# A decoder layer on one core: every call of four engines written in a new order in head, round and tail

## The chip, the cores and the metric

The kernel runs on one core of a Trainium2 chip. The metric is the device time of one execution in microseconds, the median of several. A core has five engines that run their own instruction streams in parallel: TensorE (PE), VectorE (DVE), ScalarE (ACT), GpSimd (POOL) and SyncE (SP), which here only issues transfers. They meet at semaphores: an instruction raises one when it is done, another engine waits until it has a value.

## The reference, cut to what matters

x is (4, 1024, 256), the context (4, 77, 256), all float32, and all matrices 256 x 256.

```python
# 1 self attention, sigmoid instead of softmax, q and k normalised
q, k, v = x @ Wq.T + bq, x @ Wk.T + bk, x @ Wv.T + bv
a = sigmoid(ln(q) @ ln(k).T / sqrt(256) - log(1024))
x = ln(x + ((a @ v) @ Wo.T + bo) * layerscale)
# 2 cross attention, 16 heads of 16, over 77 rows of context
p = softmax(heads(x @ wq + b) @ heads(ctx @ wk + b).T / 4)
x = ln(x + (p @ heads(ctx @ wv + b)) @ dense + b)
# 3 mix with the row before, receptance, squared keys
xp = x shifted by one row
r = sigmoid((mu_r * x + (1 - mu_r) * xp) @ W_r.T)
kk = square(relu((mu_k * x + (1 - mu_k) * xp) @ W_k.T))
out = ln(x + r * (kk @ W_v.T))
```

## The kernel before, in words

**Work and tiles.** The 4096 rows are 16 pairs of tiles (`NJ` = 16 pairs of 256 rows, `NT` = 32 tiles of 128). Self attention runs in 64 blocks of scores (`NS`), 16 for each batch. Most products are split: each operand is a high and a low half in fp32r, and `split_product` (L291) makes three matmuls of each, so that one such call on TensorE is twelve matmuls of 128x256 or six of 128x512. PSUM banks are few, and each call waits until those who read its bank before are done.

**Calls.** Each engine has one small function for each step, with its waits inside. The calls that the change and the text below speak of are:

- TensorE: `warm_up` (L1886) on zeros; `on_all_rows` (L1890), which spreads a row of biases over 128 partitions; `first_qk` (L1897), `qk` (L1929), `wvo` (L1918), the products q and k, and Wv times Wo; `tqk` (L1957), four transposes of normalised q and k; `scores` (L1971) and `attend` (L1985), twelve matmuls each; `v`, `values` (L2010); `x1` (L2022), `query` (L2030), `cross_scores` (L2039), `weights_t` (L2063, ten transposes of a tile's weights in three parts 0 to 2), `mixed` (L2076) and `dense` (L2095) of cross attention; `x2` (L2106), `receptance` (L2120), `mix_keys` (L2135) and `mix_values` of part 3.
- ScalarE: `qk_biases` (L498) and `fold_biases` (L502), which copy what `on_all_rows` made; `first_x_hi` (L484), `sigmoid` (L543), `sigmoid_hi` (L552), `exponentials` (L583, four heads a call), `mixed_hi` (L601), `query` (L575), `norm2` (L608), `v_hi` (L528). Between sigmoids and exponentials a table is loaded.
- VectorE: `first_x_lo` (L1305), `wqk_lo` (L1301), `qk_bias` (L1324), `qk_norm` (L1341, its last addition is L1347), `attended` (L1367), `stats1` (L1372), `values_bias` (L1391), `mixed_lo` (L1435), `mixes`, `mix_lo` (L1484), `gated`, `stats3` (L1508). Every low half is made at L1294.
- GpSimd: `qk_deviation` (L968), `deviation1`, `normalise` (L1045, of a tile's weights), `fold_weights`, and the like.

A chain of cross attention for one pair is: `cross_scores`, maxima (VectorE), `exponentials` (ScalarE), sums (GpSimd and VectorE), `normalise` (GpSimd), `weights_t`, copies, `mixed`, `mixed_hi` and `mixed_lo`, `dense`, then a residual and a norm.

**Order.** No scheduler is at work: each engine runs its calls in the order in which they are written. There is a head of single calls, then `for r in range(NJ): round_(r)`, in which each line is guarded by `at` (L370), so that its index must lie between two bounds, then a tail of single calls with a short loop `mix_round`. A round is one pair at every stage at once: the scores of pair r beside cross attention of pair r - 7 and q and k of tiles 2r and 2r + 1. The two lines of `at` are

```python
def at(call, i, count=NJ, first=0, *more):
    if first <= i < count:
        call(i, *more)
```

## Time and profile before

| | |
|---|---|
| three runs | 533.92, 534.5, 535.41 us; median 534.5 |
| profiled execution | 533.92 us, span of the trace 532.1 us |
| mean granted TensorE clock | 0.997 of full |
| instructions in the trace | 12650 |

The profile is of one of the runs, the fastest. Its span runs from the first to the last instruction on the core, and 1.8 us of the execution lie around it. A page gives the share of each engine; the trace behind it has every instruction with start, duration and, in brackets, the idle time of its engine just before it and the instruction that ended it. A matmul's bracket is small also where it started late, since its neighbours overlap.

### The profile page before, as it was taken

The numbers are of one execution on the slowest core, as the hardware profiler recorded it, in microseconds if no ns is written. First come the engines' busy times: TensorE is split into PE (matmuls) and PEld (weight loads), VectorE is DVE, ScalarE is ACT, GpSimd is POOL, SyncE is SP. The second block draws the span as 40 slices with busy tenths as digits, with TensorE's granted clock in tenths as the row PEclk, the third lists the DMA queues.
The fourth block names the chain that finished last, engine by engine and source line by source line (L and its number), as shares of the span: only waits on it lengthen the run. The fifth ranks groups of instructions, "written<-read, shape, count | busy, mean of one in ns | idle before, by whom it ended". The sixth has DMA issues, their size and how long they took to land.

```text
span 532.1 us, 12650 instructions
## 1 busy us (share of the span) xinstructions
PE 514.3 (97%) x4530; PEld 468.4 (88%) x4530; DVE 443.4 (83%) x995; ACT 442.7 (83%) x1070; POOL 381.6 (72%) x554
## 2 busy tenths in 40 slices
PE   9999899999999999999999999999999898999994
PEld 6799899898989898989898989999898787899994
DVE  4788868878888879797979797778878888999996
ACT  3665479897989898989898979888998799898965
POOL 1784748666857575767667675767778889897996
PEclk9999999999999999999999999999999999999998
DMA  6410010110011010101010100020601000011122
GB/s 193 127 54 30 26 60 6 41 40 2 19 44 31 30 41 22 43 19 53 10 39 2 40 2 21 21 78 24 196 5 41 2 1 1 22 41 42 41 80 100
DMA packets 23267, 22.49 MB, mean 42 GB/s; under 512 B 1723, under 2 KB 23203, under 8 KB 23204
## 3 DMA queue, kind: packets, MB, share of 16 engines
q1 hardware_dynamic: 22770, 21.35, 12.6%
q8 instruction: 36, 0.59, 0.5%
q10 hardware_dynamic: 434, 0.34, 0.2%
q14 instruction: 27, 0.22, 0.2%
HBM read 14.55 MB, written 6.82 MB: 40 GB/s over the span
## 4 chain that ended last, share of the span: by engine, by line
PE 74%; DVE 10%; ACT 8%; issue 4%; POOL 3%; POOLq 0%; DVEq 0%; ACTq 0%
PE st L296 17%; PE acc L296 15%; PE xb L296 10%; PE proj L296 9%; PE xb L2072 6%; PE xb L2091 5%; PE xb L2059 4%; DVE xm L1480 3%; ACT p_sb L590 3%; PE proj L1968 2%; PE xb L1880 1%; POOL rs L1105 1%; DVE xmT_lo L1294 1%; PE st L1888 1%; DVE kkT_lo L1294 1%
## 5 line engine op out<-in xcount | busy, mean ns | idle before, releaser
L590 ACT ACTIVATE p_sb<-xb,neg_mx 128x77 f32<-128x77 f32 x512 | 120.0, 366 | 7.7 <-DVE neg_mx L1407 7.1
L1042 POOL TENSOR_TENSOR fold<-p_sb 128x640 f32<-128x640 f32 x32 | 50.9, 1592 | 75.6 <-ACT p_sb L590 75.5
L1047 POOL TENSOR_TENSOR p_sb<-p_sb,rc 128x1280 f32<-128x1280 f32 x32 | 75.2, 2351 | 24.5 <-DVE rc L1420 24.3
L541 ACT ACT_TABLE_LOAD x58 | 74.4, 1283 | 3.2 <-issue 2.2
L296 PE MATMUL acc<-vv_hi,aT_hi 128*128 128x256 f32 x256 | 76.6, 299 | 0.0
L296 PE MATMUL st<-qkT_hi 128*128 128x256 f32 x256 | 74.8, 292 | 0.0
L296 PE MATMUL st<-qkT_lo,qkT_hi 128*128 128x256 f32 x256 | 72.4, 283 | 0.0
L296 PE MATMUL st<-qkT_hi,qkT_lo 128*128 128x256 f32 x256 | 72.4, 283 | 0.0
L296 PE MATMUL acc<-vv_lo,aT_hi 128*128 128x256 f32 x256 | 72.2, 282 | 0.0
L296 PE MATMUL acc<-vv_hi,aT_lo 128*128 128x256 f32 x256 | 72.2, 282 | 0.0
L1407 DVE TENSOR_REDUCE neg_mx<-xb 128x4 f32<-128x308 f32 x128 | 53.7, 468 | 18.0 <-PE xb L2059 17.6
L549 ACT ACTIVATE a_sb<-st,nlogs 128x512 f32<-128x512 f32 x64 | 43.7, 687 | 16.8 <-PE st L296 16.2
L296 PEld LDWEIGHTS st<-qkT_hi 128*128 128x128 f32 x256 | 48.9, 191 | 4.8 <-issue 4.2
L1427 DVE COPY pT<-xb 128x512 f32<-128x512 f32 x64 | 43.1, 676 | 11.0 <-PE xb L2072 10.9
L296 PEld LDWEIGHTS acc<-vv_hi,aT_hi 128*128 128x128 f32 x256 | 48.6, 190 | 3.4 <-issue 3.3
L2072 PE MATMUL xb<-columns,p_sb 128*128 128x128 f32 x320 | 48.4, 274 | 2.0 <-DVE pT L1427 0.6
L1294 DVE TENSOR_TENSOR aT_lo<-a_sb,aT_hi 128x512 fp32r<-128x512 f32 x64 | 47.7, 746 | 2.6 <-ACT aT_hi L475 2.2
L296 PEld LDWEIGHTS st<-qkT_lo,qkT_hi 128*128 128x128 f32 x256 | 48.9, 191 | 0.2
L296 PEld LDWEIGHTS st<-qkT_hi,qkT_lo 128*128 128x128 f32 x256 | 48.9, 191 | 0.0
L296 PEld LDWEIGHTS acc<-vv_lo,aT_hi 128*128 128x128 f32 x256 | 48.8, 191 | 0.1
L296 PEld LDWEIGHTS acc<-vv_hi,aT_lo 128*128 128x128 f32 x256 | 48.7, 190 | 0.0
L475 ACT ACTIVATE aT_hi<-a_sb 128x512 fp32r<-128x512 f32 x64 | 43.2, 678 | 2.6 <-PE acc L296 2.4
(259 smaller groups left out, 1693.1 us busy)
## 6 DMA issues: line engine op xcount, KB each, us to landing
xs<-in_x SPq DMA_DIRECT2D x16, 256.0 KB, 3.2
xraw<-in_xT SPq DMA_DIRECT2D x15, 256.0 KB, 2.9
out_y<-y SPq DMA_DIRECT2D x15, 256.0 KB, 2.1
x_kept<-xs SPq DMA_DIRECT2D x10, 256.0 KB, 2.1
x2s_a<-x_kept SPq DMA_DIRECT2D x2, 512.0 KB, 5.4
x2s_b<-x_kept SPq DMA_DIRECT2D x2, 512.0 KB, 7.2
x2s_c<-x_kept SPq DMA_DIRECT2D x1, 512.0 KB, 3.7
cT<-in_cT SPq DMA_DIRECT2D x1, 308.0 KB, 3.3
```

Source lines behind the costliest of these rows:

```text
L296: mm = pe.matmul(out, s_, m_, start=first and k == 0 and q == 0, stop=last and k == n - 1 and q == 2, skip_group_check=not check)
L475: return act.activation(out, in_, ACT.Identity, **kw)
L541: act.preload_act_table(func)
L549: act.activation(a_sb[:, i % NAR], st_bank[i % 2], ACT.Sigmoid, bias=nlogs[:, 0:1], scale=1.0 / 16).then_inc(sg_act.sem, 1)
L590: ex = act.activation(weights(t)[:, h // KH * (H // 2) + KH * n + h % KH, 0:SC], logits[n][:, h * SC:(h + 1) * SC], ACT.Exp, bias=neg_mx[: ...
L1042: pool.tensor_tensor(fold[:].rearrange("p (h k) -> p h k", k=FO), p[:, :, 0:FO], p[:, :, FO:2 * FO], ALU.add).then_inc(fo_pool.sem, 1)
L1047: pool.tensor_tensor(weights(t), weights(t), rc[:, t % 2].rearrange("p (h o) -> p h o", o=1) .to_broadcast([P, H, SP]), ALU.mult).then_inc ...
L1294: return dve.tensor_tensor(lo, whole, f(hi), ALU.subtract)
L1407: dve.tensor_reduce(neg_mx[:, t % 2, HG * n:HG * (n + 1)], logits[n][:, 0:HG * SC].rearrange("p (h k) -> p h k", k=SC), AX, ALU.min)\
L1427: dve.tensor_copy(pT[:, 4 * c:4 * c + 4, (t % 2) * P:(t % 2 + 1) * P], tiles(tp_bank(c), 4))\
L2072: mm = pe.transpose(tp_bank(c)[:, (n - 4 * c) * P:(n - 4 * c + 1) * P], p_sb[:, t % NP, n * P:(n + 1) * P], ident)
L2091: mm = pe.matmul(mixed_bank(i)[32 * n:32 * (n + 1), k * D:(k + 1) * D], vb[:, n, half, :, :, KC * b + k].rearrange("p a d -> p (a d)"), pT ...
```

## The change

No call is added, removed or altered on any engine; the functions are the same text, and SyncE's block is untouched. The order of the calls is new, in all three stretches. The head and the tail are rewritten on four engines. `at` is no longer used: `round_` has plain calls and is run for fewer rounds (TensorE 7 to 13, ScalarE 6 to 11, GpSimd 6 to 12, VectorE 5 to 10), and what lay in the rounds before and after, and in `mix_round`, is written out call by call. The cut of a round against the other engines and the order in it are new as well.

On TensorE the head begins as follows (`st`, `xb` are PSUM tiles, `brow` the row of biases, `a_sb` holds zeros in the warm-up). Before:

```order
L1888 MATMUL st<-a_sb 128x256 x4
L1888 MATMUL st<-a_sb 128x128
L1901 MATMUL xb<-wqk_hi,xT_hi 128x512 x2
L1901 MATMUL xb<-wqk_hi,xT_lo 128x512 x2
L1901 MATMUL xb<-wqk_lo,xT_hi 128x512 x2
```

The change (the same function is 285 lines further down in its file):

```order
L2173 MATMUL st<-a_sb 128x256 x4
L2173 MATMUL st<-a_sb 128x128
L2179 MATMUL st<-brow,ones 128x512 x2
L2186 MATMUL xb<-wqk_hi,xT_hi 128x512 x2
L2186 MATMUL xb<-wqk_hi,xT_lo 128x512 x2
L2186 MATMUL xb<-wqk_lo,xT_hi 128x512 x2
```

Both `on_all_rows` now stand ahead of `first_qk`; before, one came behind it and the other after `qk(3)`.

On ScalarE, in the same place (`bqk` is written by `qk_biases`, `ls` and `bo` by `fold_biases`, `xT_hi` and `wqk_hi` are high halves). Before:

```order
L541 ACT_TABLE_LOAD
L703 DMA columns<-in_columns 128x136
L475 ACTIVATE xT_hi<-xraw 128x256 x2
L475 ACTIVATE wqk_hi<-wraw 128x512
L475 ACTIVATE xT_hi<-xraw 128x512
L475 ACTIVATE bqk<-st 128x512
```

The change:

```order
L541 ACT_TABLE_LOAD
L695 DMA columns<-in_columns 128x136
L475 ACTIVATE bqk<-st 128x512
L475 ACTIVATE xT_hi<-xraw 128x256
L475 ACTIVATE ls<-st 128x256
L475 ACTIVATE bo<-st 128x256
L475 ACTIVATE xT_hi<-xraw 128x256
L475 ACTIVATE wqk_hi<-wraw 128x512
L475 ACTIVATE xT_hi<-xraw 128x512
```

The copies of biases have moved ahead of the halves of x and of the weights.

On TensorE around `mixed(13)`, at 420 us of the trace of before (`pT` are transposed weights, L2091 is `mixed`, L2059 `cross_scores`, the rows with `xmT` and `wf` are the first three of `mix_keys(0)`). Before:

```order
L2091 MATMUL xb<-pT,vb 32x256 x16
L2059 MATMUL xb<-kb,xq 128x154 x8
L296 MATMUL st<-xmT_hi,wf_hi 128x256
L296 MATMUL st<-xmT_lo,wf_hi 128x256
L296 MATMUL st<-xmT_hi,wf_lo 128x256
```

The change (L2357 is `weights_t`, L2165 the transposes of `x2(1)`, L2376 `mixed`):

```order
L2357 MATMUL xb<-columns,p_sb 128x128 x10
L2165 MATMUL proj<-columns,x2s_a 128x128 x4
L2376 MATMUL xb<-pT,vb 32x256 x16
L296 MATMUL st<-xmT_hi,wf_hi 128x256
L296 MATMUL st<-xmT_lo,wf_hi 128x256
L296 MATMUL st<-xmT_hi,wf_lo 128x256
```

`cross_scores(29)` now follows behind all twelve matmuls of `mix_keys(0)`.

The diff, cut to the places above and those that the prediction speaks of: the head and the round of ScalarE, the end of VectorE's tail, and of TensorE the round, the head, the stretches around `tqk(9)`, `weights_t(0, .)` and `mixed(13)`.

```diff
                 def round_(r):
-                    at(xt_hi, r + 3, NJ, 9)
-                    at(weights_tail, 2 * r - 9, NTA, 3)
-                    at(sigmoid, 4 * r - 7, NS, 16)
-                    at(mixed_hi, r - 5, NJ, 1)
-                    at(sigmoid, 4 * r - 6, NS, 16)
-                    at(exponentials, 2 * r - 7, NT, 4, 0)
-                    at(exponentials, 2 * r - 7, NT, 4, 1)
-                    at(exponentials, 2 * r - 7, NT, 4, 2)
-                    at(sigmoid_hi, 4 * r - 7, NS, 16)
-                    at(exponentials, 2 * r - 7, NT, 4, 3)
-                    at(norm1, r - 3, N1, 3)
-                    at(sigmoid_hi, 4 * r - 6, NS, 16)
-                    at(tqk_hi, 2 * r + 4, NT, 15)
-                    at(x1_hi, r - 3, NJ, 3)
-                    at(sigmoid, 4 * r - 5, NS, 16)
-                    at(v_hi, r + 2, NJ, 7)
-                    at(norm2, r - 6, N2)
-                    at(weights_tail, 2 * r - 8, NTA, 3)
-                    at(sigmoid, 4 * r - 4, NS, 16)
-                    at(query, r - 3, NJ, 2)
-                    at(sigmoid_hi, 4 * r - 5, NS, 16)
-                    at(exponentials, 2 * r - 6, NT, 4, 0)
-                    at(exponentials, 2 * r - 6, NT, 4, 1)
-                    at(sigmoid_hi, 4 * r - 4, NS, 16)
-                    at(exponentials, 2 * r - 6, NT, 4, 2)
-                    at(tqk_hi, 2 * r + 5, NT, 15)
-                    at(exponentials, 2 * r - 6, NT, 4, 3)
-
-                def mix_round(i):
-                    at(key_squares, i - 1, NJ, 22)
-                    at(mix_hi, i + 1, NJ, 24)
-                    at(key_relu, i, NJ, 22)
-                    at(gate_sigmoid, i - 1, NJ, 19)
-                    at(carried, i + 7, NJ, 17)
-
+                    exponentials(2 * r - 7, 1)
+                    exponentials(2 * r - 7, 2)
+                    norm1(r - 3)
+                    exponentials(2 * r - 7, 3)
+                    tqk_hi(2 * r + 4)
+                    sigmoid_hi(4 * r - 6)
+                    x1_hi(r - 3)
+                    sigmoid(4 * r - 5)
+                    norm2(r - 6)
+                    weights_tail(2 * r - 8)
+                    sigmoid_hi(4 * r - 5)
+                    v_hi(r + 2)
+                    query(r - 3)
+                    sigmoid(4 * r - 4)
+                    exponentials(2 * r - 6, 0)
+                    exponentials(2 * r - 6, 1)
+                    sigmoid_hi(4 * r - 4)
+                    exponentials(2 * r - 6, 2)
+                    tqk_hi(2 * r + 5)
+                    xt_hi(r + 4)
+                    exponentials(2 * r - 6, 3)
+                    weights_tail(2 * r - 7)
+                    sigmoid(4 * r - 3)
+                    sigmoid_hi(4 * r - 3)
+                    mixed_hi(r - 4)
+                    sigmoid(4 * r - 2)
+                    exponentials(2 * r - 5, 0)
...
                 table_for(ACT.Sigmoid)
                 act.dma_start(columns[:], io["columns"]).then_inc(load_id.sem, 16)
+                qk_biases()
                 first_x_hi(0)
+                fold_biases()
                 first_x_hi(1)
                 wqk_hi(1)
                 xt_hi(1)
-                qk_biases()
                 xt_hi(2)
-                fold_biases()
                 qk_norm(0)
+                wvo_hi()
                 tqk_hi(0)
+                xt_hi(3)
                 qk_norm(1)
-                wvo_hi()
-                xt_hi(3)
...
-                for r in range(NJ):
...
+                for r in range(6, 12):
                     round_(r)
...
                 mixes(14)
-                key_squares_lo(11)
-                stats3(9)
+                key_squares_lo(12)
                 mix_lo(14)
-                gated(10)
+                stats3(10)
                 gated(11)
-                stats3(10)
-                key_squares_lo(12)
+                key_squares_lo(13)
+                gated(12)
+                mixes(15)
+                mix_lo(15)
                 stats3(11)
-                mixes(15)
-                gated(12)
-                key_squares_lo(13)
-                mix_lo(15)
                 key_squares_lo(14)
                 gated(13)
                 stats3(12)
                 gated(14)
+                stats3(13)
                 key_squares_lo(15)
-                stats3(13)
@@ -2164,281 +2449,327 @@
                     mm.then_inc(fv_pe.sem, 1)
 
                 def round_(r):
-                    at(attend, 4 * r - 18, NS, 9)
-                    at(scores, 4 * r - 15, NS, 13)
-                    at(weights_t, 2 * r - 13, NT, 1, 0)
-                    at(tqk, 2 * r - 1, NT, 13)
-                    at(weights_t, 2 * r - 13, NT, 1, 1)
-                    at(attend, 4 * r - 17, NS, 9)
-                    at(weights_t, 2 * r - 13, NT, 0, 2)
-                    at(qk, 2 * r, NT, 14)
-                    at(mixed, r - 7)
-                    at(scores, 4 * r - 14, NS, 13)
-                    at(cross_scores, 2 * r - 11, NT, 2)
-                    at(v, r, NJ, 7)
-                    at(scores, 4 * r - 13, NS, 13)
-                    at(scores, 4 * r - 12, NS, 13)
-                    at(dense, r - 7)
-                    at(weights_t, 2 * r - 12, NT, 1, 0)
-                    at(tqk, 2 * r, NT, 13)
-                    at(x1, r - 5, NJ, 2)
-                    at(attend, 4 * r - 16, NS, 9)
-                    at(qk, 2 * r + 1, NT, 14)
-                    at(weights_t, 2 * r - 12, NT, 1, 1)
-                    at(weights_t, 2 * r - 12, NT, 0, 2)
-                    at(query, r - 5, NJ, 1)
-                    at(attend, 4 * r - 15, NS, 9)
-                    at(cross_scores, 2 * r - 10, NT, 2)
-
-                def mix_round(i):
-                    at(mix_keys, i - 3, NJ, 12)
-                    at(mix_values, i - 5, NJ, 14)
-                    at(receptance, i - 3, NJ, 14)
-                    at(x2, i, NJ, 18)
...
-
+                    weights_t(2 * r - 13, 0)
+                    tqk(2 * r - 1)
+                    weights_t(2 * r - 13, 1)
+                    attend(4 * r - 17)
+                    weights_t(2 * r - 13, 2)
+                    qk(2 * r)
+                    mixed(r - 7)
+                    scores(4 * r - 14)
+                    cross_scores(2 * r - 11)
+                    v(r)
+                    scores(4 * r - 13)
+                    scores(4 * r - 12)
+                    dense(r - 7)
+                    tqk(2 * r)
+                    weights_t(2 * r - 12, 0)
+                    x1(r - 5)
+                    weights_t(2 * r - 12, 1)
+                    attend(4 * r - 16)
+                    qk(2 * r + 1)
+                    weights_t(2 * r - 12, 2)
+                    query(r - 5)
+                    attend(4 * r - 15)
+                    cross_scores(2 * r - 10)
+                    attend(4 * r - 14)
+                    scores(4 * r - 11)
 
                 warm_up()
+                on_all_rows(0)
+                on_all_rows(1)
                 first_qk()
-                on_all_rows(0)
                 qk(2)
                 qk(3)
-                on_all_rows(1)
+                wvo()
+                tqk(0)
                 qk(4)
-                tqk(0)
...
+                attend(3)
+                scores(5)
                 values(1)
-                tqk(8)
-                keys(1)
-                scores(4)
-                qk(9)
-                attend(1)
-                attend(2)
-                attend(3)
+                scores(6)
                 tqk(9)
-                scores(5)
+                scores(7)
                 qk(10)
-                scores(6)
+                x1(0)
                 v(5)
-                scores(7)
-                x1(0)
...
+                cross_scores(1)
                 scores(10)
                 qk(12)
-                cross_scores(1)
-                attend(7)
                 scores(11)
                 v(6)
+                weights_t(0, 0)
+                attend(8)
+                weights_t(0, 1)
+                x1(1)
+                tqk(12)
+                attend(9)
+                query(1)
+                weights_t(0, 2)
+                qk(13)
                 scores(12)
-                attend(8)
-                tqk(12)
-                weights_t(0, 0)
-                x1(1)
-                weights_t(0, 1)
-                qk(13)
-                for r in range(NJ):
+                cross_scores(2)
+                scores(13)
+                attend(10)
+                for r in range(7, 14):
                     round_(r)
+                weights_t(15, 0)
...
                 cross_scores(28)
-                x2(1)
-                attend(62)
+                attend(63)
                 weights_t(27, 0)
                 weights_t(27, 1)
                 weights_t(27, 2)
-                attend(63)
+                x2(1)
                 mixed(13)
+                mix_keys(0)
                 cross_scores(29)
-                mix_keys(0)
                 receptance(0)
-                dense(13)
-                x1(15)
                 weights_t(28, 0)
                 weights_t(28, 1)
-                x2(2)
+                x1(15)
+                dense(13)
                 query(15)
                 weights_t(28, 2)
+                x2(2)
...
```

## Rows read from the trace of the kernel before

**Rows 1.** The page, part 1: busy time, share of the span, instructions of each engine.

```profile
PE 514.3 (97%) x4530; PEld 468.4 (88%) x4530; DVE 443.4 (83%) x995; ACT 442.7 (83%) x1070; POOL 381.6 (72%) x554
```

**Rows 2.** 20 us windows: us; busy (x instructions) PE, PEld, DVE, ACT, POOL; PEclk, DMA, GB/s.

```profile
40.00:60.00 20.00, 18.57 (x131) 16.80 (x130) 16.43 (x31) 8.39 (x15) 10.54 (x18) 1.00 0.11 35
...
420.00:440.00 20.00, 16.64 (x167) 14.26 (x166) 16.64 (x40) 16.05 (x53) 17.77 (x23) 1.00 0.01 2
...
500.00:520.00 20.00, 18.90 (x152) 18.12 (x151) 18.79 (x44) 15.37 (x31) 18.97 (x33) 1.00 0.20 67
520.00:532.00 12.00, 5.08 (x41) 4.73 (x39) 7.16 (x23) 6.49 (x12) 7.64 (x17) 0.87 0.32 110
```

**Rows 3.** Chain of waits: start us, us, what; `mixed` in it.

```profile
103.15 1.90 PE xb L2091 x32
...
129.05 1.90 PE xb L2091 x32
...
336.41 1.90 PE xb L2091 x32
...
420.35 1.94 PE xb L2091 x32
```

**Rows 4.** Timeline around `tqk(9)`, TensorE, then VectorE: start us, us, operation, [idle before <-releaser].

```profile
55.06 0.28 PE L296 MATMUL acc<-vv_lo,aT_hi 128*128 128x256 f32 x1
55.18 0.28 PE L296 MATMUL acc<-vv_hi,aT_lo 128*128 128x256 f32 x1
56.80 0.44 PE L1968 MATMUL proj<-columns,qk_sb 128*128 128x128 f32 x2 [1.35 <-DVE qk_sb L1347]
...
51.19 0.69 DVE L1329 TENSOR_TENSOR qk_sb<-proj,bqk 128x512 f32<-128x512 f32 x1 [1.43 <-PE proj L296]
...
52.80 1.11 DVE L1395 TENSOR_TENSOR v<-xb,bxv 77x256 f32<-77x256 f32 x2
```

**Rows 5.** Timeline of TensorE from `mixed(13)` on.

```profile
423.78 0.81 PE L2059 MATMUL xb<-kb,xq 32*128 32x154 f32 x16 [1.53 <-DVE oT_lo L1294]
424.52 0.39 PE L296 MATMUL st<-xmT_hi,wf_hi 128*128 128x256 f32 x1
...
429.49 0.60 PE L1880 MATMUL xb<-columns,xs 128*128 128x128 f32 x4
...
434.13 0.81 PE L2059 MATMUL xb<-kb,xq 32*128 32x154 f32 x16 [0.72 <-ACT xq L475]
```

**Rows 6.** Head: timeline of TensorE, then the tiles `brow` and `wraw`.

```profile
5.18 1.19 PE L1901 MATMUL xb<-wqk_hi,xT_hi 128*128 128x512 f32 x2
...
8.74 1.12 PE L1894 MATMUL st<-brow,ones 1*128 1x512 f32 x2
...
18.60 0.58 PE L296 MATMUL xb<-wqk_hi,xT_first_hi 128*128 128x512 f32 x1
...
L701 ACTq DMA_DIRECT2D brow<-in_brow x1: 537/537/537, 1.6 to 1.6; - x1
...
DMA to landing us min/median/max: 3.0/3.5/4.3
```

**Rows 7.** Line L1347, the last addition of `qk_norm`: ns min/median/max.

```profile
L1347 DVE TENSOR_TENSOR qk_sb<-qk_sb,nb x26: 691/693/1762, 32.6 to 331.3; 128x512 f32<-128x512 f32 x26
```

**Rows 8.** Timeline of ScalarE and TensorE before `cross_scores` in a repeated round.

```profile
275.00 0.84 ACT L475 ACTIVATE xq<-xb,columns 128x256 f32<-128x256 f32 x2
...
276.31 0.81 PE L2059 MATMUL xb<-kb,xq 32*128 32x154 f32 x16
```

**Rows 9.** Timeline of TensorE, `weights_t` behind a `cross_scores` that starts at 350.96.

```profile
353.80 0.41 PE L2072 MATMUL xb<-columns,p_sb 128*128 128x128 f32 x2 [0.41 <-ACT p_sb L590]
```

**Rows 10.** Timeline of VectorE in the tail.

```profile
513.61 0.74 DVE L1515 BATCH_NORM_STATS2 st<-y 128x6 f32<-128x256 f32 x2
514.27 0.30 DVE L1520 BATCH_NORM_AGGREGATE mv<-st 128x2 f32<-128x6 f32 x2
...
517.28 1.28 DVE L1294 TENSOR_TENSOR xmT_lo<-xm,xmT_hi 128x512 fp32r<-128x512 f32 x2
```

More of the change, by code:

```diff
@@ new lines, in _ @@
+                tqk_hi(29)
+                sigmoid(45)
+                weights_tail(17)
+                v_hi(14)
+                norm2(6)
+                sigmoid(46)
+                sigmoid_hi(45)
+                mixed_hi(8)
+                norm1(10)
+                sigmoid_hi(46)
+                exponentials(19, 0)
+                exponentials(19, 1)
+                exponentials(19, 2)
+                exponentials(19, 3)
+                x1_hi(10)
+                tqk_hi(30)
+                sigmoid(47)
@@ L810, in _ @@
+                exponentials(24, 1)
+                exponentials(24, 2)
+                exponentials(24, 3)
                 sigmoid(57)
@@ L812, in _ @@
                 sigmoid_hi(57)
+                sigmoid(58)
+                sigmoid_hi(58)
                 exponentials(25, 0)
@@ new lines, in _ @@
+                tqk(28)
+                weights_t(16, 1)
+                dense(7)
+                weights_t(16, 2)
+                x1(9)
+                scores(44)
+                attend(41)
+                query(9)
+                qk(29)
+                cross_scores(18)
+                scores(45)
+                attend(42)
+                weights_t(17, 0)
+                attend(43)
+                tqk(29)
+                weights_t(17, 1)
+                weights_t(17, 2)
+                scores(46)
@@ L2272, in _ @@
+                qk(30)
+                mixed(8)
+                v(15)
+                attend(44)
+                cross_scores(19)
+                scores(47)
+                scores(48)
+                weights_t(18, 0)
+                attend(45)
+                x1(10)
+                weights_t(18, 1)
+                tqk(30)
+                weights_t(18, 2)
+                dense(8)
+                query(10)
+                qk(31)
+                cross_scores(20)
                 attend(46)
+                weights_t(19, 0)
@@ L2300, in _ @@
                 mixed(10)
-                attend(52)
+                scores(54)
                 cross_scores(23)
```

1141 lines of the change are left out of this document (718 added, 423 removed).

## Prediction

> **What bounds the kernel now.** I read the page's engine shares first: TensorE is busy 97% of the span, no other engine over 83% [rows 1]. A new order removes no work, so it can only remove time in which TensorE stands still. The 20 us windows say where: 1.43 us at 40 to 60, 3.36 at 420 to 440, 1.10 at 500 to 520, and 6.92 in the last 12 us, where TensorE's work thins out [rows 2]. In the chain of waits the same call, `mixed`, comes back after 25.9 us (103.15 to 129.05): that is the repeated round [rows 3].
>
> The windows understate the standstill. A matmul of 0.28 us is followed by the next after 0.12, so twelve take 1.44, and each late start hides 0.16 us under the matmul before: `tqk(9)` starts 1.62 us after the last matmul of `attend(3)`, and shows 1.35 idle [rows 4]. Between `mixed(9)` (336.41) and `mixed(13)` (420.35) lie 83.9 us [rows 3]. Their calls at full pace: 37 of twelve matmuls, 53.3; 4 `mixed`, 7.6; 8 `cross_scores` at 0.74 (423.78 to 424.52), 5.9; 22 sets of four transposes at 0.44 (0.60 busy less the 0.16 under the next) and 8 pairs at half of it, 11.4 [rows 5]; some 0.18 for each of 12 changes to and from mixed or cross_scores, 2.1; less 0.4, since dense and query are a little shorter. That is 79.9, so 4 us are waiting though the windows show far less. Summed in this way over the program, waiting comes to some 19 us beside the start and the last 7 us.
>
> The Trainium skill (Perfetto Trace Analysis, Identifying the Most-Contended Engine) calls matmul busy time a poor measure of headroom and asks for the weight-load share instead. Here that share is 88%, which would leave 12% or 64 us; the pace of 0.12 us per matmul leaves a third of that, and I go by the pace.
>
> **The change, part by part.** The same calls stand on every engine, with 58 table loads as before, so added work costs nothing. The sum is made against the profiled execution, 533.9 us (span 532.1), which is 0.6 below the median of 534.5.
>
> *Head, to 20 us.* Both `on_all_rows` (1.05 us each; the first is 8.74 to 9.79) move ahead of `first_qk` on TensorE, and on ScalarE the two bias copies go ahead of the halves of x. The row they need (`brow`) is issued at 1.6; the weights on the same queue took 3.0 to 4.3 us to land, so it is there by 5.9 at worst, against 5.18, the end of the warm-up [rows 6]. TensorE then starts `first_qk` at about 7.3, not 5.18. VectorE now makes both low halves of x before the low part of the first weights, and has the second weights' low part at about 10.1, so `first_qk` ends at about 10.7 instead of 8.74. The 2.1 us of `on_all_rows` are by then done, as is the wait for the first biases. Adding `qk(2)`, `qk(3)`, `wvo`, `tqk(0)` and `qk(4)` at full pace (1.4, 1.4, 2.5, 0.45, 1.5) gives 18.0; before, that set ended at 18.60 [rows 6]. Gain 0.5 (bounds -0.7, if the row lands at its worst, and 1.2). Between 20 and 50 us half of some 0.7 of small waits may go: 0.3.
>
> *tqk(9).* It waited for `qk_norm(9)`: VectorE takes the result of `qk(9)` at 51.19, 0.2 us after TensorE ends it, and `tqk(9)` starts at 56.80, so 5.8 us after `qk(9)` [rows 4]. Before, 4.3 us of attend covered this; now `attend(3)`, `scores(5)`, `values(1)` and `scores(6)` do, 4 x 1.44 and the changes between them, 6.2 us. On VectorE `attended(0)` and `stats1(0)` come into the chain (some 1.6 us, one addition and the statistics at the paces of this stretch) and `values_bias(0)` (1.1) leaves it. One of the 26 last additions of `qk_norm` took 1.76 where 0.69 is usual, and it is the one that TensorE waited for [rows 7]. So the chain is 6.3 us with the slow addition, 5.2 with a usual one. So 0 to 0.1 is left. Gain 1.6 (0.5 to 2). Later `weights_t(0,0)` and `(0,1)` no longer stand so close: a wait of 0.3 goes, an estimate from the sum of standstill at 80 to 100 us.
>
> *Repeated round.* Three rows change places on TensorE (`tqk` before `weights_t(.,0)`, and `weights_t(.,1)` two calls earlier). Nothing waited there, so no gain, and I find nothing new that is late: 0. The least cover is ScalarE's `query` copies, done at 275.84 for `cross_scores` at 276.31, 0.47 us [rows 8].
>
> *336 to 420 us.* Each `cross_scores` is followed by 2.3 us of TensorE work before a `weights_t` that wants its exponentials 2.8 us after its start; at 353.80 this shows as 0.41 idle, so 0.57 late [rows 9]. The new order puts two calls instead of one behind `cross_scores(24)`, `(25)` and `(27)`, and leaves one behind `(22)`, `(26)` and `(28)`. I count 0.6 each as left on those three plus 0.8 of small ones, 2.6 of 4.2: gain 1.6 (0 to 3).
>
> *mixed(13).* `cross_scores(29)` waited 1.53 for the chain mixed, `mixed_hi`, `mixed_lo` [rows 5]. `mix_keys(0)` (1.5) now stands between. But next are `weights_t(28,.)`, moved ahead of `dense(13)`, which want `normalise(28)` and `exponentials(29,1)`. With the normalise two small groups earlier on GpSimd these come some 5.3 and 4.8 us after mixed's end, TensorE is there after 3.9: 1.4 comes back. `dense(13)` then covers the halves of x1. I reach `cross_scores(30)` 10.9 us after mixed's end instead of 11.95 (422.18 to 434.13): gain 1.1 (0 to 3).
>
> *Tail.* VectorE is busy 18.79 of 20 us at 500 to 520, TensorE 18.90 [rows 2]: the two set the pace together, and VectorE's work is unchanged. What can go is order: `stats3(11)` (0.74 and 0.30, at 513.61) moves behind `mix_lo(15)` (517.28), which `mix_keys(15)` waits for [rows 10], 1.0 us sooner. With the last 7 us as before: gain 1.2 (0 to 3.5).
>
> Sum: 0.5 + 0.3 + 1.6 + 0.3 + 1.6 + 1.1 + 1.2 = 6.6. 533.9 - 6.6 is 527.3; the runs' median is 0.6 above the profiled run, so half a microsecond more: **527.8 us**.
>
> **Rivals.**
> - *Waits come back later.* ScalarE and VectorE set the pace from 340 us on, so TensorE, sooner at one call, waits at the next. For: VectorE's 18.79 us from 500. Against: ScalarE idles 4.0 us and VectorE 3.4 at 420 to 440 [rows 2]. Only the first 100 us gain: 2.7, so 531.7.
> - *Nearly all waits go.* The upper ends of the bounds: 1.2 + 0.7 + 2 + 0.3 + 3 + 3 + 3.5 = 13.7, so 520.7.
> - *No change.* The order does little: counts per round are equal, and head and tail give back what tqk(9) gains. 533 to 535.
> - *Slower: the round's cover fails.* ScalarE's order around `v_hi`, `norm2` and `query` is new. If the query copies end over 0.47 us later, each of ten rounds stands still. If they end 1.3 us later, 0.85 a round is lost and ten rounds cost 8.5: 6.6 is eaten up and 1.9 added, 536.3. It decides from 0.8 of standstill a round, where the sum passes the 533.9 of before by over 1.6. For: the small cover. Against: the copies swapped (`sigmoid_hi` for `sigmoid`) last the same.
> - *Slower: VectorE beside GpSimd.* One addition in 26 took 1.07 us more than the median of 0.69 [rows 7]. If the new order lays eight more such subtractions and additions beside GpSimd's work, where TensorE waits for them, 8 x 1.07 = 8.6 cancels the gain: 536.4. For: nothing in the order says which way the pairs fall. Against: the one that TensorE waited for goes or stays alone, and elsewhere the cover is over 1 us. The Trainium skill (SBUF — State Buffer, Who interferes with whom) has the second port as an exclusive lock for VectorE instructions with two SBUF inputs against GpSimd's reads. By that rule this time is one instruction waiting for the other; the slow one agrees with it.
>
> **How the numbers follow.** About 0.3%, 1.6 us, is what a measurement of this kernel can tell from no change, so faster is below 532.9. Forecast 0.53, waits come back 0.20, nearly all go 0.05 (all faster, 0.78); no change 0.13; the query copies 0.05, VectorE beside GpSimd 0.04 (slower, 0.09). Eight in ten: from 522.8 (between forecast and the low rival) to 533.0 (past the first rival).
>
> **What would show it.** Right: TensorE's idle at 40 to 60 us near 0.2; the round still 25.9 us; `cross_scores(29)` without wait but `weights_t(28,0)` with one of about a microsecond; `mixed(13)` 3.5 to 5 us earlier than 420.3; 7 us still behind the last matmul. Wrong: a round of 26.2 or more, a `first_qk` ending after 11.5, or VectorE with more busy time than 443 us. The forecast falls if the sum of waiting from 420 on is unchanged.

## The result and the profile after

| | before | the change |
|---|---|---|
| median of 4 runs each | 534.21 us (533.58 to 535.41) | **542.05 us** (540.68 to 542.84) |
| ratio | | 1.0141, 95% interval 1.0110 to 1.0173 |
| profiled execution, span | 533.92, 532.1 | 542.83, 541.0 |

The change is 1.4% slower. I had forecast 527.8 us, 1.2% faster, with a chance of 0.09 for slower: direction and range were both wrong.

Part 1 of the page of the changed kernel, in answer to [rows 1]:

```profile
PE 517.9 (96%) x4530; PEld 470.4 (87%) x4530; DVE 455.8 (84%) x995; ACT 442.8 (82%) x1070; POOL 383.9 (71%) x554
```

The number of instructions on each engine is the same, and VectorE is busy 12.4 us longer with them. The prediction named more than 443 us on VectorE as a sign against it.

Windows of the changed kernel (columns as in [rows 2]):

```profile
0.00:20.00 20.00, 17.25 (x42) 11.47 (x43) 9.02 (x21) 5.67 (x11) 4.60 (x15) 1.00 0.42 128
...
40.00:60.00 20.00, 20.00 (x152) 18.97 (x151) 15.47 (x29) 9.11 (x16) 16.13 (x17) 1.00 0.14 41
420.00:440.00 20.00, 17.83 (x177) 15.64 (x176) 18.45 (x43) 16.86 (x53) 18.42 (x19) 1.00 0.08 27
500.00:520.00 20.00, 20.00 (x168) 19.80 (x168) 19.80 (x50) 18.23 (x39) 19.11 (x36) 1.00 0.15 53
```

Where the change was meant to help, at 40 to 60 and at 500 to 520, TensorE has no idle time left. The loss lies where I had put nothing. The chain of waits, whose pieces of `mixed` answer to [rows 3]:

```profile
106.57 1.90 PE xb L2376 x32
...
132.58 1.90 PE xb L2376 x32
...
158.46 1.89 PE xb L2376 x32
...
185.28 1.90 PE xb L2376 x32
...
212.11 1.89 PE xb L2376 x29
...
238.94 1.90 PE xb L2376 x32
...
265.78 1.90 PE xb L2376 x32
...
292.64 1.90 PE xb L2376 x32
```

The round lasts 26.0 and 25.9 us at first, then 26.8: some 0.9 more in each of five rounds. Standstill summed as in the prediction, by the start of each call less the full pace of its kind, gives the account (us, the change less before):

| stretch | predicted | measured |
|---|---|---|
| head, to the end of `qk(4)` (18.60 before, 23.68 now) | -0.5 | +5.1 |
| from there to 160 | -2.2 | -1.3 |
| 160 to 340, the repeated rounds | 0 | +6.1 (6.2 against 0.1) |
| 340 to 460 | -2.7 | +0.5 (11.7 against 11.2) |
| 460 to the last matmul | -1.2 | -1.0 (3.0 against 4.1) |
| last matmul to the end | 0 | -0.1 |

The rows add up to 9.3, against 8.9 in the spans. Of the 6.1 in the rounds 4.6 are the five rounds of 26.8; the rest lies at 300 to 340. Some 0.7 of it is `tqk(28)`, which waits for the last such addition: from `mixed(7)` to `mixed(8)` the change takes 28.2 us, and 27.5 with that addition short (e1 below). For the other half of the rest no cause is shown.

**A round of the changed kernel.** The timeline of VectorE, GpSimd, ScalarE, and of TensorE without its split matmuls:

```profile
192.24 0.68 DVE L1478 TENSOR_TENSOR qk_sb<-qk_sb,rs 128x512 f32<-128x512 f32 x1
192.96 1.82 DVE L1480 TENSOR_TENSOR qk_sb<-qk_sb,nb 128x512 f32<-128x512 f32 x1
194.70 0.68 DVE L1427 TENSOR_TENSOR aT_lo<-a_sb,aT_hi 128x512 fp32r<-128x512 f32 x1
195.31 0.46 DVE L1540 TENSOR_REDUCE neg_mx<-xb 128x4 f32<-128x308 f32 x1
...
192.40 0.58 POOL L1091 TENSOR_TENSOR nbl<-nbl,rsl 128x2 f32<-128x2 f32 x1
192.93 1.29 POOL L1056 TENSOR_TENSOR xT_lo<-xraw,xT_hi 128x512 fp32r<-128x512 f32 x1
...
195.80 0.97 ACT L590 ACTIVATE p_sb<-xb,neg_mx 128x77 f32<-128x77 f32 x4 [1.29 <-DVE neg_mx L1540]
...
195.70 0.60 PE L2357 MATMUL xb<-columns,p_sb 128*128 128x128 f32 x4
196.92 0.63 PE L2165 MATMUL xb<-columns,xs 128*128 128x128 f32 x4 [0.62 <-ACT p_sb L590]
```

GpSimd's `nbl`, of 128x2, takes 0.58 instead of 0.20: it ends when VectorE's L1478 ends. GpSimd then starts `xt_lo` (L1056) 0.03 us ahead of VectorE's next addition, and that takes 1.82 instead of 0.69: it ends 0.56 after GpSimd's instruction. The two engines hand each other the turn, and they meet like this, 0.02 to 0.03 us apart, in six rounds; in a seventh GpSimd came second. Behind the slow addition now stand a low half of scores and `maxima(., 3)` (L1540); ScalarE waits 1.29 us for it, and `x1` on TensorE starts 0.79 us late. Before, `maxima(., 3)` stood ahead of `qk_norm`, and `xt_lo` behind `residual2`.

Line L1480 in the changed kernel, against [rows 7], says the same of its longest; seven of the 26 took 1.67 to 1.82:

```profile
L1480 DVE TENSOR_TENSOR qk_sb<-qk_sb,nb x26: 691/693/1822, 36.5 to 342.0; 128x512 f32<-128x512 f32 x26
```

**The head.** TensorE, VectorE and GpSimd in the changed kernel, against [rows 6]:

```profile
5.31 3.78 PE L2179 MATMUL st<-brow,ones 1*128 1x512 f32 x4
9.02 1.22 PE L2186 MATMUL xb<-wqk_hi,xT_hi 128*128 128x512 f32 x2
10.04 1.05 PE L2186 MATMUL xb<-wqk_hi,xT_lo 128*128 128x512 f32 x2
12.67 1.22 PE L2186 MATMUL xb<-wqk_lo,xT_hi 128*128 128x512 f32 x2 [1.58 <-DVE wqk_lo L1427]
13.69 1.05 PE L2186 MATMUL xb<-wqk_hi,xT_hi 128*128 128x512 f32 x2
...
10.12 0.83 DVE L1427 TENSOR_TENSOR xT_lo<-xraw,xT_hi 128x256 fp32r<-128x256 f32 x1 [1.34 <-ACT xT_hi L475]
10.87 2.35 DVE L1427 TENSOR_TENSOR wqk_lo<-wraw,wqk_hi 128x512 fp32r<-128x512 f32 x2
...
10.62 1.44 POOL L1048 TENSOR_TENSOR wo_ls<-wo_ls,ls 128x512 f32<-128x512 f32 x1
```

Three things come together: each `on_all_rows` takes 1.85 us and not 1.05; the second half of x waits on ScalarE behind both bias copies; and the low half of the weights, late by that, meets GpSimd's fold of the output weights (L1048): two low halves take 2.35 us, where two of this size elsewhere take 1.3. The matmuls come 0.43 to 0.51 us apart (0.85 to 1.02 for two), up to the start of `qk(2)` at 16.25, where before they came 0.23 apart from 6.8 on. 512 columns in 0.43 us is the level of 1.2 GHz, in 0.23 that of 2.4. In this profile the column of the granted clock shows 1.00 in all of the stretch and does not tell the two apart; in e7, e6 and e2 below it shows 0.50 where the matmuls come 0.43 apart.

### The profile page after: what moved, and what is told of

It is laid out like the page before. It is cut to its first block, busy times and chain, and to the rows that moved or that the text cites. A ratio compares the mean times of both kernels' runs of the same rounds, so it can differ in the third digit from the quotient of the medians.

```text
span 541.0 us, 12658 instructions
## 1 busy us (share of the span) xinstructions
PE 517.9 (96%) x4530; PEld 470.4 (87%) x4530; DVE 455.8 (84%) x995; ACT 442.8 (82%) x1070; POOL 383.9 (71%) x554
## 3 DMA queue, kind: packets, MB, share of 16 engines
q1 hardware_dynamic: 22770, 21.35, 12.5%
## 4 chain that ended last, share of the span: by engine, by line
PE 80%; DVE 10%; issue 4%; ACT 3%; POOL 2%; DMA 1%; POOLq 0%; DVEq 0%; ACTq 0%
PE st L296 19%; PE acc L296 18%; PE xb L296 12%; PE proj L296 8%; PE xb L2357 5%; PE xb L2376 5%; PE xb L2344 4%; DVE neg_mx L1540 2%; PE xb L2165 2%; PE proj L2253 2%; ACT p_sb L590 1%; DVE aT_lo L1427 1%; DVE pT L1560 1%; PE st L2173 1%; DVE v_sb L1493 1%
## 5 line engine op out<-in xcount | busy, mean ns | idle before, releaser
L590 ACT ACTIVATE p_sb<-xb,neg_mx 128x77 f32<-128x77 f32 x512 | 117.4, 361 | 15.3 <-DVE neg_mx L1540 15.0
L1137 POOL TENSOR_TENSOR p_sb<-p_sb,rc 128x1280 f32<-128x1280 f32 x32 | 75.2, 2351 | 27.5 <-DVE rc L1553 27.5
L1540 DVE TENSOR_REDUCE neg_mx<-xb 128x4 f32<-128x308 f32 x128 | 55.4, 467 | 16.3 <-PE xb L2344 15.7
L2357 PE MATMUL xb<-columns,p_sb 128*128 128x128 f32 x320 | 49.4, 274 | 4.7 <-DVE pT L1560 1.9
L1427 DVE TENSOR_TENSOR aT_lo<-a_sb,aT_hi 128x512 fp32r<-128x512 f32 x64 | 53.0, 829 | 0.2 <-ACT aT_hi L475 0.2
L2357 PEld LDWEIGHTS xb<-columns,p_sb 128*128 128x128 f32 x320 | 37.0, 140 | 8.3 <-DVE pT L1560 2.9
```

Of the source, the lines that this page charges most:

```text
L590: ex = act.activation(weights(t)[:, h // KH * (H // 2) + KH * n + h % KH, 0:SC], logits[n][:, h * SC:(h + 1) * SC], ACT.Exp, bias=neg_mx[: ...
L1137: pool.tensor_tensor(weights(t), weights(t), rc[:, t % 2].rearrange("p (h o) -> p h o", o=1) .to_broadcast([P, H, SP]), ALU.mult).then_inc ...
L1427: return dve.tensor_tensor(lo, whole, f(hi), ALU.subtract)
L1540: dve.tensor_reduce(neg_mx[:, t % 2, HG * n:HG * (n + 1)], logits[n][:, 0:HG * SC].rearrange("p (h k) -> p h k", k=SC), AX, ALU.min)\
L2357: mm = pe.transpose(tp_bank(c)[:, (n - 4 * c) * P:(n - 4 * c + 1) * P], p_sb[:, t % NP, n * P:(n + 1) * P], ident)
```

## The experiments

Each is the changed kernel, or the kernel before, with a few calls moved; no call is added, and none computes anything else. The kernel before was run beside them each time: medians 534.2, 534.12 and 533.75 us.

**e1: GpSimd's `xt_lo` back.**

```diff
                     deviation1(r - 3)
-                    xt_lo(r + 3)
                     fold_weights(2 * r - 7)
                     deviation2(r - 6)
                     residual2(r - 4)
+                    xt_lo(r + 3)
```

> The changed kernel, with xt_lo(r + 3) in GpSimd's round moved from behind deviation1 to behind residual2, where it stood before. Theory port: in the changed kernel xt_lo starts 0.02 to 0.03 us ahead of VectorE's last addition of qk_norm, which then takes 1.82 us instead of 0.69; maxima(., 3) stands behind it, then exponentials(., 3), then TensorE's x1, which starts 0.79 us late in six rounds. With xt_lo later the addition takes 0.69 again and the wait before x1 is gone: about 4.6 us less, 542.05 to 537.4; from 160 to 300 us TensorE's standstill falls from 4.7 to under 1 us. Rival order: x1 waits because ScalarE's and VectorE's order in the round put the exponentials late, whatever GpSimd does: no change, 542. Rival later: xt_lo behind residual2 makes q and k late instead: over 542.

Measured 537.24 us, 4.8 less than the change. The longest L1480 is 0.818 us, the round lasts 25.9, and of TensorE's waits at 160 to 330 us (3.1 for the exponentials before `x1`, 0.3 for the addition) none is left. Rows of e1, VectorE:

```profile
191.37 0.68 DVE L1478 TENSOR_TENSOR qk_sb<-qk_sb,rs 128x512 f32<-128x512 f32 x1
192.08 0.69 DVE L1480 TENSOR_TENSOR qk_sb<-qk_sb,nb 128x512 f32<-128x512 f32 x1
```

**e2: VectorE's `maxima(., 3)` back, GpSimd as changed.**

```diff
                     maxima(2 * r - 3, 2)
+                    maxima(2 * r - 3, 3)
                     qk_norm(2 * r + 8)
                     sigmoid_lo(4 * r + 1)
-                    maxima(2 * r - 3, 3)
```

> The changed kernel, with maxima(., 3) in VectorE's round put ahead of qk_norm and of the low half of the scores, where it stood before; GpSimd as in the changed kernel. Theory port with an exposed place: the addition of qk_norm still takes 1.8 us in some six rounds, but nothing that TensorE waits for stands behind it in the next microsecond: x1 on time, 537.4. Theory port alone (every such collision costs its 1.1 us wherever it lies): 542. If the low half of the scores, which now is late, is what attend wants, the wait only changes its place: 540 to 543.

Measured 536.74 us. Six additions are as slow as before the edit, and `x1` no longer waits behind them: the round lasts 25.9 us. Of the waits for an addition only that of `tqk(28)` stays, 0.6. Rows of e2, VectorE, GpSimd and TensorE:

```profile
191.18 1.67 DVE L1480 TENSOR_TENSOR qk_sb<-qk_sb,nb 128x512 f32<-128x512 f32 x1
...
190.51 1.80 POOL L1056 TENSOR_TENSOR xT_lo<-xraw,xT_hi 128x512 fp32r<-128x512 f32 x1
...
193.98 0.60 PE L2165 MATMUL xb<-columns,xs 128*128 128x128 f32 x4
```

Here GpSimd came second to L1478 (190.47) and took 1.80 instead of 1.29, then VectorE came second to it. So in these rounds a collision costs only where something due stands behind it: e1 takes the collision away, e2 its victim, and either is enough.

**e3: the head back.**

```diff
 tensor
-                on_all_rows(0)
-                on_all_rows(1)
                 first_qk()
+                on_all_rows(0)
+                on_all_rows(1)
 scalar
-                qk_biases()
                 first_x_hi(0)
-                fold_biases()
                 first_x_hi(1)
                 wqk_hi(1)
                 xt_hi(1)
+                qk_biases()
+                fold_biases()
 vector
                 first_x_lo(0)
-                first_x_lo(1)
                 wqk_lo(0)
+                first_x_lo(1)
```

> The changed kernel, with the bias copies of ScalarE behind the high halves of x and of the weights, both on_all_rows behind first_qk on TensorE, and VectorE's first low halves in the order of before. All else as changed. Theory head: the order in the first 20 us costs 5.1 us (the set of calls up to qk(4) ends at 23.7 instead of 18.6) and nothing behind takes it back: first_qk starts at 5.2, ends at 8.7, 542.05 becomes 537. Rival slack: what is won in the head is waited for at 30 to 70 us, where q, k and the norms limit: 540 to 542.

Measured 537.69 us, 4.4 less than the change. `qk(2)` starts at 10.55 and not 16.25, `mixed(0)` at 100.99 and not 106.50: the change never made the head's loss good, and what is won back reaches the end: the spans of the two profiled executions differ by 5.8 us. The medians differ by 4.4 only; the last section has a reason why they may fall short, TensorE's pace in the head.

**e7: as e3, but `on_all_rows` stays first on TensorE.** The edit is e3 without its first part, so ScalarE's and VectorE's calls go back together, and what each of them does is not told apart.

> As e3, but both on_all_rows stay ahead of first_qk on TensorE; ScalarE's and VectorE's order in the head as before. Theory ScalarE's queue: what cost the head was that the halves of x waited behind the bias copies; with those behind, only the matmuls of on_all_rows themselves stand in front: first_qk starts at 7.5 to 9.0, runs without a gap, qk(2) starts at 11 to 12.5, and the time is 538 to 539. Theory TensorE's pace: matmuls stay at the slow pace until late, as in the changed kernel (qk(2) at 16.25), because of what TensorE did first: first_qk from 9.0 at 0.5 us a matmul, ends at 14.2, time 541.

Measured 538.73 us, 1.0 more than e3, 3.3 less than the change; `qk(2)` starts at 11.23. So the larger part of the head's loss is the order on ScalarE and VectorE with what follows from it, and by the medians 1 us is TensorE's. Its four runs lie apart, though (537.66, 537.88, 539.59, 540.40), and the profile is of that of 537.88. TensorE in e7, then the window from 8 to 11 us:

```profile
4.88 1.98 PE L2179 MATMUL st<-brow,ones 1*128 1x512 f32 x4
6.79 0.73 PE L2186 MATMUL xb<-wqk_hi,xT_hi 128*128 128x512 f32 x2
7.36 0.68 PE L2186 MATMUL xb<-wqk_hi,xT_lo 128*128 128x512 f32 x2
7.84 1.06 PE L2186 MATMUL xb<-wqk_lo,xT_hi 128*128 128x512 f32 x2
...
8.00:11.00 3.00, 3.00 (x9) 2.35 (x8) 0.90 (x2) 1.73 (x5) 1.75 (x2) 0.50 0.56 173
```

Its matmuls were 0.24 us apart by 7.4, and from 7.84 to 11.2 again 0.43, without any gap, at a granted clock of 0.50. What stood between the warm-up and the fall were the one-row matmuls of `on_all_rows` and four others. It is not shown that their new place is the cause. In e3, with `first_qk` ahead of them, the pace did not fall; in e6 (below), whose head is that of e3, it fell from 12.23 to 15.2 us, 1.3 us behind the same one-row matmuls. TensorE in e6, then the window from 12.5 to 15 us:

```profile
12.23 0.63 PE L296 MATMUL xb<-wqk_hi,xT_lo 128*128 128x512 f32 x1
12.65 0.63 PE L296 MATMUL xb<-wqk_hi,xT_hi 128*128 128x512 f32 x1
...
12.50:15.00 2.50, 2.50 (x7) 1.91 (x7) 2.21 (x7) 0.00 (x0) 2.42 (x6) 0.50 0.01 4
```

**e4, e12, e11: the two edits of the round in the kernel before,** one by one and together. A 2 by 2 test in a program that has none of the rest of the change.

```diff
 gpsimd (e4, e11)
                     at(deviation1, r - 3, NJ, 1)
+                    at(xt_lo, r + 3, NJ, 7)
...
                     at(residual2, r - 4)
-                    at(xt_lo, r + 3, NJ, 7)
 vector (e12, e11)
                     at(sigmoid_lo, 4 * r - 3, NS, 17)
+                    at(maxima, 2 * r - 5, NT, 4, 3)
...
                     at(stats2, r - 4)
-                    at(maxima, 2 * r - 3, NT, 4, 3)
```

(After the last round `maxima(27, 3)` is called once more by itself.)

> The kernel before, with xt_lo(r + 3) in GpSimd's round put directly behind deviation1, as the change has it; VectorE as before, so with maxima(., 3) ahead of qk_norm. Theory port with an exposed place: one of qk_norm's two operations takes 1.8 us instead of 0.69 in each of some eight rounds, but no wait of TensorE comes of it: 534 to 535. Theory port alone: eight rounds by 0.8 to 1.1, 541 to 543. Rival: GpSimd's order decides nothing, no slow additions, 534.

> The control for e11: the kernel before with VectorE's edit alone. Without the collision maxima(., 3) ends at about 268.5 and the exponentials at 269.6, beside x1 at 269.5: 0 to 0.3 us a round, 534 to 537. Together with e4 (GpSimd's edit alone, 535.98) and e11 this shows whether the two edits cost more together than apart.

> The kernel before with both edits of the round: GpSimd's xt_lo directly behind deviation1, and VectorE's maxima(., 3) behind qk_norm and the low half of the scores that follow it. Theory port with an exposed place: exponentials(., 3), then x1, come later by the whole of it. From the trace of before, maxima(., 3) would end at about 268.5 and not 265.4 without the collision and at 269.6 with it, exponentials 1.1 us after that at 270.7, and x1 is due at 269.5: 1.2 us a round, for the six or seven rounds in which both are there 7 to 8 us: 541 to 543. Rival: the collision does not matter, only VectorE's order: same as e12.

| | GpSimd as before | `xt_lo` early |
|---|---|---|
| VectorE as before | 534.2; round 25.9 | e4: 535.98; round 25.9 |
| `maxima(., 3)` late | e12: 546.55; round 27.1 | e11: 553.07; round 27.6 |

(The round is from `mixed(4)` to `mixed(5)`.) In e4 a collision in every round (the first step of `qk_norm` takes 1.65 instead of 0.70) costs nothing there, as expected; the 1.8 us came at 80 to 140 us, from single waits. Together the edits cost 19.3 us, 4.7 more than apart (1.8 and 12.8). That is the interaction I claim for the change. But the size of e12 was a miss: I had looked for 0 to 0.3 us a round, and it was 1.15; e11, for which I had named 541 to 543, came out 10 us above that for the same reason. I had reckoned with the exponentials alone and left out what stands behind them on ScalarE. In the kernel before that is `norm1`, and `x1` waits for it. TensorE in e12, then in e11, one round each:

```profile
194.63 0.66 PE L1882 MATMUL xb<-columns,xs 128*128 128x128 f32 x4 [0.92 <-ACT xs L475]
```

```profile
199.02 0.66 PE L1882 MATMUL xb<-columns,xs 128*128 128x128 f32 x4 [1.50 <-ACT xs L475]
```

The changed kernel has `norm1` ahead of `exponentials(., 3)`, and the late `maxima` alone (e1) cost it nothing. That the place of `norm1` is why is a reading of the two orders; no run moved it alone.

**e5: e2 and e3 together.**

> The changed kernel with the edits of e2 and e3 together: biases behind the halves of x in the head, maxima(., 3) ahead of qk_norm in the round. If the two causes are independent, their gains add (5.3 and 4.4 us): 532.3, which is under the kernel before. If both gains are one slack in different places (the rounds catch up what the head lost), 536 to 537.

Measured 533.03 us, ratio to before 0.9985 (0.9975 to 0.9995). The two causes are 9.0 us together, 9.7 by their sum: nearly independent (the edit of e2 is worth 5.3 by itself and 4.7 on top of e3). With both undone the rest of the change is worth 1.1 us against the kernel before.

**e6: three swaps on VectorE in the middle.**

```diff
-                rest_of_mu()
                 weights_tail(23)
+                rest_of_mu()
...
+                x1_lo(13)
                 sigmoid_lo(58)
                 crossed(11)
                 weights_tail(24)
-                x1_lo(13)
...
-                wf_split(0)
                 weights_body(25, 0)
                 maxima(26, 3)
                 weights_tail(25)
                 weights_body(25, 1)
+                wf_split(0)
```

> As e5, with three swaps on VectorE at 380 to 410 us: rest_of_mu (1.42 us) behind weights_tail(23) and not ahead of it, x1_lo(13) ahead of the low half of scores 58 and crossed(11), wf_split(0) behind the copies of weights 25. Theory place: TensorE's waits before mixed(11) (0.95), query(13) (1.08) and weights_t(25, 2) (1.0) in e3 are each made by one VectorE operation that nobody needs yet and that stands ahead of one that TensorE waits for: these go, some is waited for later, 2 us less than e5: 530.3. Rival chain: the middle is bound by the chain of cross attention over three engines, and the waits move to the next call: same as e5 within 0.5.

Measured 534.94 us, 1.9 worse than e5. The three waits shrank or went, and TensorE then waited for `xq` (0.8) and 2.1 for one low half, both before a `cross_scores`. In the waits of e6 at 380 to 420 us:

```profile
PE xb L2344 <- DVE oT_lo L1427: 2.1, 1, 2.1
PE xb L2344 <- ACT xq L475: 0.8, 1, 0.8
```

`wf_lo`, moved by the third swap, had met GpSimd's `fold_weights` and taken 1.94 us, and a low half of scores behind it had met `residual2` and taken 1.66. Much of the 1.9 us is not of the middle. In the profiled executions e6 is 2.6 us longer than e5, and 1.4 of that is there at the end of `qk(4)`, in a head of the same code, where the granted clock fell to 0.50. All twelve runs of e6 have a mean granted clock of 0.990 to 0.994; the three runs of e5 that reach only 0.992 to 0.995 took 534.08 to 534.40, against 534.94. So the swaps themselves cost some 0.5 to 1.2 us, and gained nothing: the reading that the waits move is the nearer one. Which of the three swaps did what was not tried.

**e8: the swap around `mixed(13)`, alone, in the kernel before.**

```diff
                 mixed(13)
-                cross_scores(29)
                 mix_keys(0)
+                cross_scores(29)
                 receptance(0)
```

> The kernel before with one swap on TensorE: mix_keys(0) between mixed(13) and cross_scores(29). By my prediction's reading of the change 1.53 us of standstill before cross_scores(29) go and part of it comes back. Theory gain: 1 us less, 533.2. Theory moved: cross_scores(29) starts at 423.7 as before, 1.44 us of work less stands between it and dense(13), which wants its exponentials, and dense(13) waits 1.5 us longer: 534.2, no change, the whole wait moved.

Measured 534.82 us, ratio 1.0017 (1.0007 to 1.0027). TensorE in e8:

```profile
424.13 0.81 PE L2059 MATMUL xb<-kb,xq 32*128 32x154 f32 x16
...
428.33 0.39 PE L296 MATMUL xb<-wx_hi,oT_hi 128*128 128x256 f32 x1 [1.77 <-ACT p_sb L590]
...
434.50 0.81 PE L2059 MATMUL xb<-kb,xq 32*128 32x154 f32 x16 [0.72 <-ACT xq L475]
```

The 1.53 us before `cross_scores(29)` of [rows 5] are gone, and `dense(13)` waits 1.77 instead of 0.31. `cross_scores(30)` starts 12.0 us after the end of `mixed(13)`, as it did before. All of the wait moved.

**e9: e5 with the tail mended.** In the changed kernel the last call of TensorE waits; TensorE and VectorE:

```profile
532.39 0.38 PE L296 MATMUL xb<-wf_hi,kkT_hi 128*128 128x256 f32 x1 [1.87 <-DVE kkT_lo L1427]
...
530.20 0.69 DVE L1637 SCALAR_TENSOR_TENSOR y<-gate,acc 128x512 f32<-128x512 f32 x1 [1.48 <-DMA out_y<-y]
...
531.68 0.66 DVE L1427 TENSOR_TENSOR kkT_lo<-xb,kkT_hi 128x512 fp32r<-128x512 f32 x1
```

```diff
+                key_squares_lo(15)
                 gated(14)
                 stats3(13)
-                key_squares_lo(15)
```

> As e5, with key_squares_lo(15) ahead of gated(14) and stats3(13) at the end of VectorE's tail. In e5 the last call of TensorE, mix_values(15), waits some 1.9 us for that low half, which stands behind gated(14), held by a transfer of y that isn't out. Theory place: mix_values(15) starts at once, and the end is 1.5 to 2 us earlier: 531.3. Rival end: the last rows wait for the norms of rows 12 to 14 on GpSimd and ScalarE or for their transfers, and the end moves under 0.5: 532.7.

Measured 532.43 us, 0.9973 of before (0.9962 to 0.9984), so 0.6 less than e5 by the ratios. `mix_values(15)` starts 2.3 us earlier (520.24), but then the statistics of row pair 14 wait 1.18 us for GpSimd's `y`, and the last norm is only 1 us earlier. Between the two theories, nearer to the second.

**e10: e9 and e1's edit.**

> As e9, with GpSimd's xt_lo(r + 3) behind residual2 as in e1. Slow additions in the rounds fall from 7 to 2, but since maxima(., 3) is out of their way nothing waited for them: theory port with an exposed place says the same time as e9 within 0.5 us, 531.3. Theory port alone says 4 to 6 us less. If a low half of scores was late behind the slow addition at 280 to 300 us (0.87 standstill in e5), 0.9 less: 530.4.

Measured **531.37 us**, 0.9950 of before (0.9937 to 0.9962), 1.1 less than e9: the last reading held as a difference to e9, which itself had come out above its forecast. From `mixed(7)` to `mixed(8)` e9 takes 28.2 us and e10 27.4. It is the fastest kernel of the study, 0.5% under the kernel before and some 10 us under the change, and differs from the change by five moved calls in the head, two in the round and one in the tail.

## Why the prediction was wrong

- **Where TensorE stands still:** right. The account by full pace, made again on the changed kernel, found all of the loss (9.3 us against 8.9 in the spans), also where the windows showed little.
- **Head, predicted -0.5, measured +5.1.** Two steps failed. One is "has the second weights' low part at about 10.1": it was there at 13.2. The second half of x waited on ScalarE behind both bias copies, and then VectorE's low halves met GpSimd's fold, which those copies had started. By e7 this order is the larger part, 3.3 of 4.4 us. The other is the price of both `on_all_rows` and of what follows them. I took 1.05 us from the row at 8.74 [rows 6], which stands at 2.4 GHz; the place they moved to can be at 1.2, as `first_qk` at 5.18 in the same rows shows (1.19 us for two matmuls, against 0.62 later). In the profile of the change each took 1.85, and `first_qk` kept that pace to its end at 16.25, against the 10.7 of the prediction; in those of e2 and e7 they took 1.1 and 0.95. My bound of -0.7 was far too near. e3 undoes the loss: 4.4 us.
- **`tqk(9)`, predicted -1.6 with a range from 0.5 to 2:** right in mechanism. TensorE's idle time at 40 to 60 us is 0.00, where I had named 0.2 as the sign.
- **Repeated round, predicted 0, measured +6.1.** The step: "I find nothing new that is late: 0". I read TensorE's and ScalarE's order there, where the least cover was 0.47 us, and not what VectorE and GpSimd do side by side. The rival "VectorE beside GpSimd" had the mechanism, its price (1.07 us each; here 1.0 to 1.13) and nearly the count (eight; here seven additions of `qk_norm`, and six low halves of scores beside `residual2`), at a chance of 0.04. What I held against it, that elsewhere the cover is over 1 us, was said of the order of before. The new order had taken that cover away by putting `maxima(., 3)` behind. It could have been read from the two orders: two moves on two engines, each of which the changed kernel bears by itself (e1, e2).
- **336 to 420 us and `mixed(13)`, predicted -2.7, measured +0.5.** `cross_scores(29)` does start without wait, and `weights_t(28, 0)` waits 1.62 us, as foretold. The step that failed is "gain 1.1" beside it: e8, the same swap in the kernel before, shows that all of the wait moves. In the stretch ahead of it I counted only calls of TensorE; VectorE's `rest_of_mu` (1.42 us), `wf_split(0)` and a low half of 2.03 us beside GpSimd now stood ahead of what TensorE wanted. That these three are the cause is read from the rows; when e6 moved them, the waits went to other calls and no time was won.
- **Tail, predicted -1.2, measured -1.0:** right in size. Of the standstill at 500 to 520 nothing shows in the window now (idle 1.10 before), and a new wait of 1.87 before `mix_values(15)` takes part of that back.

The signs that I had named against the forecast (a round of 26.2 or more, `first_qk` ending after 11.5, VectorE over 443 us) all came: 26.8, 16.25 and 455.8. `mixed(13)`, foretold 3.5 to 5 us earlier than 420.3, came at 431.75.

## What to carry to other kernels

When an order of several engines is rewritten, check for each engine what now stands directly behind an instruction that can be stretched, and whether someone is due on it: a collision that was harmless under the old order can be exposed by a move on another engine. Take the price of a moved instruction from rows at the place that it moves to, clock included. Count a removed wait as a gain only when the next two calls have been given their due times as well; e8 and e6 show waits of 1 to 2 us that only went to the next call.

## What the runs showed of the hardware

**VectorE and GpSimd take turns.** With additions, subtractions or products of two SBUF tensors on VectorE (`aT_lo`, `xmT_lo`, both steps of `qk_norm`) beside GpSimd's tensor-tensor instructions, the one that starts first keeps its own time, and the other ends some 0.5 us after it. VectorE second: started 0.03, 0.46 and 1.0 us after a GpSimd instruction of 1.29 it took 1.82, 1.38 and 0.84. GpSimd second: the same instruction took 1.74 to 1.80. GpSimd's scalings of one tensor (L1097, L1156 in the change) stretched no such subtraction by more than 0.25. A cast is not safe either: `wf_hi`, with one input in SBUF, took 1.49 us beside `xs<-xs,bo` at 407.1 in the changed kernel, and 0.41 at 428.7. The Trainium skill (SBUF — State Buffer, Who interferes with whom) says that the order of issue decides which engine blocks; every pair looked at here agrees. Then there is the hand-over: a 128x2 instruction of GpSimd that had been held up (0.58 instead of 0.20) set the next one free at the very moment of VectorE's next, round after round.

**TensorE's pace in the head varies between executions with the same head.** In the profiled execution of e2, with the changed head, both `on_all_rows` took 2.2 us together (5.31 to 7.51) and not 3.7, the first matmuls of `first_qk` ran at 2.4 GHz, and after 2.25 us of waiting the next ones, from 10.96 to 15.4, at 1.2 again, with a granted clock of 0.50:

```profile
8.08 0.63 PE L2186 MATMUL xb<-wqk_hi,xT_lo 128*128 128x512 f32 x2
10.96 1.22 PE L2186 MATMUL xb<-wqk_lo,xT_hi 128*128 128x512 f32 x2 [2.25 <-DVE wqk_lo L1427]
```

That makes 1.7 us up to `qk(2)`, and may be the spread of 2.2 us among the four runs of the change, of which only one has a profile. Their mean granted clocks fit it: 0.998 in both runs of 542.8, and 0.989 and 0.992 in those of 541.27 and 540.68; in e7 it is 0.998 in the two long runs and 0.994 in the two short ones. The lower mean goes with the shorter time here, and the profiles say how: in those of e2, e6 and e7 a slow stretch behind one at 2.4 GHz shows as 0.50, while in that of the change, where the matmuls come 0.43 us apart from 9.02 on, the column stays at 1.00. So medians of few runs mix two heads: with runs of like clock compared, e2's edit is worth 4.3 us (536.45 to 536.74 against 540.68 and 541.27) and e1's 5.5 (537.21 to 537.74 against 542.8), where the medians give 5.3 and 4.8. A cost under 2 us in the first 20 us needs more than one profile.
